# Earlier sums of squares in the handover, and four score banks with head-by-head maxima in the softmax attention of a language-model tower

## The reference

```python
hx = layernorm(h)
q, k, v = heads(hx @ Wq), heads(hx @ Wk), heads(hx @ Wv)      # 2 heads of 64
q = l2norm(q) * sqrt(64) * qn_g ;  k = l2norm(k) * sqrt(64) * kn_g
scores = where(causal, q @ k.T / sqrt(64), smallest)
o = softmax(scores) @ v ;  y = merge(o) @ Wo
gate = softmax(y @ gate_W + gate_b)                            # 8 experts
hid = gelu(y @ W1 + b1) ;  eo = hid @ W2 + b2                  # all experts, dense
out = h + sum(gate * eo)
```

## Time and profile before

| what | value |
|---|---|
| three runs | 873.12, 876.09, 878.2 us; median 876.09 |
| profiled execution, its own time | 872.14 us |
| its span | 870.3 us |
| busy shares of the span | PE 90%, DVE 82%, ACT 55%, POOL 39% |
| the chain that ended last | PE 78%, DVE 9%, issue 6%, ACT 5% |

### The profile page before, as it was taken

One profiled execution on the slowest core, in us unless ns is written; L12 is line 12 of the kernel. 1 busy time (PEld: TensorE's weight loads), 2 busy tenths in 40 slices (PEclk: granted clock), 3 DMA queues, 4 the chain that ended last, 5 costly groups with the idle time before them and its releaser, 6 DMA issues.

```text
span 870.3 us, 20958 instructions
## 1 busy us (share of the span) xinstructions
PE 785.4 (90%) x8188; PEld 556.7 (64%) x8188; DVE 709.8 (82%) x1588; ACT 479.3 (55%) x997; POOL 338.7 (39%) x379
## 2 busy tenths in 40 slices
PE   2699999999756688899999979999999999999997
PEld 1568887788523355555555556677777777777775
DVE  3558899888557766677676887999999999999997
ACT  2435555555234556677688865555555555555553
POOL 6639999777444456566467750000000000000000
PEclk9799999999879999999999999999999999999999
DMA  3101111000000000000000000000000000000000
GB/s 127 55 8 29 27 37 37 25 26 26 0 1 0 1 2 2 2 2 3 2 2 15 2 2 2 2 14 2 14 2 14 2 14 2 14 2 14 1 14 14
DMA packets 9666, 12.09 MB, mean 14 GB/s; under 512 B 1856, under 2 KB 6592, under 8 KB 9568
## 3 DMA queue, kind: packets, MB, share of 16 engines
q1 hardware_dynamic: 8544, 8.65, 3.4%
q0 software_dynamic: 1024, 2.10, 0.9%
HBM read 8.65 MB, written 2.10 MB: 12 GB/s over the span
## 4 chain that ended last, share of the span: by engine, by line
PE 78%; DVE 9%; issue 6%; ACT 5%; DMA 1%; POOL 1%; another core or an unknown queue 0%; DVEq 0%; ACTq 0%; POOLq 0%
PE ps L977 76%; DVE mx L825 1%; ACT qk L483 1%; ACT room L553 1%; DVE room L930 1%; DVE qkn L779 1%; DVE room L928 1%; ACT room L544 1%; DMA h_all<-emb_rows,idx 1%; DVE v L770 1%; DVE ss L764 1%; PE ps L1005 1%; DVE mx L820 1%; PE ps L985 0%; DVE och L901 0%
## 5 line engine op out<-in xcount | busy, mean ns | idle before, releaser
L568 ACT ACTIVATE cst<-ps,col 128x512 f32<-128x512 f32 x256 | 175.9, 688 | 164.1 <-PE ps L977 163.4
L977 PEld LDWEIGHTS ps<-arena,sq 128*128 128x128 f16 x3072 | 192.1, 98 | 61.8 <-DVE sq L961 4.3
L977 PE MATMUL ps<-arena,sq 128*128 128x128 f16 x3072 | 213.0, 219 | 0.5 <-DVE sq L961 0.5
L977 PE MATMUL ps<-y,arena 128*128 128x512 f16 x768 | 208.6, 381 | 1.3 <-DVE och L901 1.3
L961 DVE TENSOR_TENSOR sq<-cst,sq 128x512 f16<-128x512 f32 x256 | 176.2, 688 | 4.5
L364 POOL TENSOR_TENSOR room<-room 128x512 f16<-128x512 f32 (+3 forms) x119 | 121.1, 1034 | 82.3 <-ACT room L553 82.0
L956 DVE CAST sq<-cst 128x512 f16<-128x512 f32 x256 | 109.3, 427 | 11.6 <-ACT cst L568 4.2
L544 ACT ACTIVATE room<-ps 128x512 f32<-128x512 f32 (+3 forms) x160 | 76.7, 532 | 44.2 <-PE ps L977 42.9
L825 DVE TENSOR_REDUCE mx<-ps 128x2 f32<-128x1024 f32 (+2 forms) x64 | 70.2, 1096 | 37.6 <-PE ps L977 37.5
L977 PEld LDWEIGHTS ps<-y,arena 128*128 128x128 f16 x768 | 65.0, 98 | 34.2 <-issue 3.9
L977 PEld LDWEIGHTS ps<-v,room 128*128 128x128 f16 x1632 | 59.5, 99 | 40.5 <-issue 26.0
(11 more groups left out here) (154 smaller groups left out, 1172.6 us busy)
## 6 DMA issues: line engine op xcount, KB each, us to landing
sq<-w_rows SPq DMA_DIRECT2D x16, 256.0 KB
out<-h_all SPq DMA_DIRECT2D x32, 64.0 KB, 1.6
cst<-consts SPq DMA_DIRECT2D x1, 896.0 KB
h_all<-emb_rows,idx POOLq DMA_INDIRECT x32, 5.1
cst<-consts SPq DMA_DIRECT2D x1, 398.0 KB, 3.4
c<-consts SPq DMA_DIRECT2D x1, 256.0 KB, 5.5
wqkv<-w_qkv SPq DMA_DIRECT2D x1, 192.0 KB
wsm<-w_sm SPq DMA_DIRECT2D x1, 192.0 KB, 5.5
```

The lines of the kernel that those rows point to most:

```text
L568: a.activation(hid[:, f], ps[:, HBANK[f], :], ACT.Gelu_apprx_tanh, bias=col[:, K_B1 + k:K_B1 + k + 1], scale=1.0 / WS).then_inc(S["hid_rea ...
L977: return t_.matmul(o, l, r, start=start, stop=stop, skip_group_check=True)
```

## The change

In the handover DVE's step c now takes `sum_squares(c+1)` straight behind `unit_qk(c)`, where `sum_squares(c+2)` stood at the end of the step; `low_v(c+1)` stands last. POOL's factors follow at one chunk ahead, the coefficients of the last chunk are split by sequence into two groups of four (8 columns each, at c = 1 and 2), and the second masked product of that chunk goes ahead of `sum_squares(0)`. Pieces that finish the last chunk move one step later.

In the attention the exact scores go round four banks, 0, 1, 2, 5. All items are in `ALONE`: from item 3 on every head's rough scores go into bank 3, one after the other, with a reduction each, 128 in all in place of 64. `max_row` and the chain move to bank 4 (the last item's chain to 5). DVE takes a step's maxima ahead of its other work, and has 38 subtractions where it had 41: 20 in odd steps 19 to 61 with one part, 18 in the last 18 steps.

The core of the diff, which leaves out the waits that carry `bank5` over to a table `free` by bank:

```diff
@@ GpSimd @@
-                if c + 2 < NT:
-                    l2_factors(c + 2)
-                if c == 1:
-                    coefs(NT - 1)
+                if c + 1 < NT:
+                    l2_factors(c + 1)
+                if c in (1, 2):
+                    last_coefs(c - 1)
@@ ScalarE @@
-                        a.activation(p32[:, i % QR, lo:], ps[:, i % 3, lo:], ACT.Exp).then_inc(S["s_used"], 1)
+                        a.activation(p32[:, i % QR, lo:], ps[:, SBANK[i % 4], lo:], ACT.Exp).then_inc(S["s_used"], 1)
@@ VectorE @@
+            masked(NT - 1, 1)
             sum_squares(0)
-            masked(NT - 1, 1)
...
             def step_b(c):
                 unit_qk(c)
+                if c + 1 < NT:
+                    sum_squares(c + 1)
+                if c == 0:
+                    h1_out(NT - 2)
                 if c + 3 < NT:
                     normed2(c + 3)
-                if c == 0:
-                    sum_squares(1)
-                    low_v(1)
-                    h1_out(NT - 2)
...
-                if c + 2 < NT:
-                    sum_squares(c + 2)
-                    low_v(c + 2)
+                if c + 1 < NT:
+                    low_v(c + 1)
...
-                for part in MSLOT.get(s, ())[:1]:
+                two = MSLOT.get(s, ())
+                for part in two if two and two[0][0] > 2 else two[:1]:
                     row_max(*part, (0, 1))
@@ TensorE @@
             def lone_scores(it, r, kb, w, k, h):
...
-                if g < 10:
-                    pe.wait_ge(S["lo_ready"], NT - 1)
-                else:
-                    pe.wait_ge(S["sm_used"], g - 1)
+                pe.wait_ge(*free[bank])
...
-                guard = S["sm_used"], g + 1
+                free[bank] = S["sm_used"], g + 1
...
-                if s:
-                    pe.wait_ge(S["s_used"], 2 * s - 1)
+                if s >= 2:
+                    pe.wait_ge(S["s_used"], 2 * s - 2)
...
-                for part in lone[1:2]:
+                for part in lone[1:2] if len(lone) > 2 else ():
                     lone_scores(*part)
-                for part in pairs[:1]:
-                    pair_scores(*part)
                 if LAG <= s < NSTEP + LAG:
                     values(s - LAG, 1)
-                for part in lone[2:]:
+                for part in lone[2:3] if len(lone) > 2 else lone[1:]:
                     lone_scores(*part)
...
-                for part in pairs[1:]:
-                    pair_scores(*part)
+                for part in lone[3:]:
+                    lone_scores(*part)
@@ tables @@
-ALONE = (1, 2)
+ALONE = tuple(range(1, 8))
+SBANK = [0, 1, 2, 5]
+def chain_bank(m):
+    return 5 if m == len(ITEMS) - 1 else 4
+def lone_bank(it, g):
+    return 3 + g % 2 if it <= 2 else 3
```

More of the change, by code:

```diff
@@ L273, in coefs, with last_coefs @@
                                 ALU.subtract).then_inc(S["coef"], 1)
+            def last_coefs(b):
+                n = NT + b
+                pool.wait_ge(S["var_ready"], NT)
+                g.tensor_tensor(sm[:, 4, b], sm[:, 3, b], mhalf[:, 0:HA], ALU.pow).then_inc(S["r_ready"], 1)
+                pool.wait_ge(S["r_ready"], n)
+                g.tensor_tensor(sm[:, 5, b], sm[:, 4, b], row[:, R_NG:R_NG + HA], ALU.mult).then_inc(S["gr_ready"], 1)
+                pool.wait_ge(S["gr_ready"], n)
+                g.tensor_tensor(sm[:, 6, b], sm[:, 5, b], sm[:, 0, b], ALU.mult).then_inc(S["grmu_ready"], 1)
+                pool.wait_ge(S["grmu_ready"], n)
+                g.tensor_tensor(sm[:, 7, b], row[:, R_NB:R_NB + HA], sm[:, 6, b], ALU.subtract).then_inc(S["coef"], 1)
             def weights_low(n):
@@ L533, in out_part @@
                     act.wait_ge(S["gT_ps"], m + 1)
[L534 removed]
+                    a.activation(gT[:], ps[0:4 * E, chain_bank(m), 0:P], ACT.Copy, scale=WS).then_inc(S["gT_sb"], 1)
             max_row(0)
@@ L674, in outputs @@
             def outputs(c, cur, first=False):
-                dve.wait_ge(S["coef"], c + 1)
+                dve.wait_ge(S["coef"], c + 1 if c < NT - 1 else NT + 1)
                 dve.wait_ge(S["x_sb"], 2 * c + 2)
@@ L917, in _ @@
                         head_out(it)
+                for m in range(LAST):
+                    if s - YAT[m] in DVE_Y[:2]:
+                        out_part(m, DVE_Y.index(s - YAT[m]) + 3)
                 for i in (2 * s, 2 * s + 1):
@@ L931, in _ @@
                                         ).then_inc(S["plo_dve"], 1)
[L932 to L936, removed]
+                if two[1:] and two[0][0] <= 2:
+                    row_max(*two[1], (0, 1))
             dve.wait_ge(S["wlow_ready"], NPIECE)
@@ L1213, in lone_scores @@
                 if it == 2 and (r, kb) == (0, 0):
                     pe.wait_ge(S["hi_ready"], NT)
-                last = mm(ps[:, 3 + g % 2, 0:w], qh[half, q:q + P], kh[half, at:at + w], stop=kb < c)
+                last = mm(ps[:, bank, 0:w], qh[half, q:q + P], kh[half, at:at + w], stop=kb < c)
                 if kb == c:
                     for z in range(2):
-                        last = mask(ps[:, 3 + g % 2, w - P:w], z, h, neg_qk)
+                        last = mask(ps[:, bank, w - P:w], z, h, neg_qk)
@@ L1271, in scores @@
                         half = slice(h * DS, (h + 1) * DS)
-                        mm(ps[:, (2 * s + h) % 3, lo:], still[half, at:at + P], moving[half, q0 + lo:q0 + CH],
+                        mm(ps[:, SBANK[(2 * s + h) % 4], lo:], still[half, at:at + P], moving[half, q0 + lo:q0 + CH],
                            start=still is kh and moving is qh, stop=False)
@@ L1281, in scores @@
                     half = slice(h * DS, (h + 1) * DS)
-                    last = mm(ps[:, (2 * s + h) % 3, lo:], onehot[half], qm[half, it % 2, lo:], start=False)
+                    last = mm(ps[:, SBANK[(2 * s + h) % 4], lo:], onehot[half], qm[half, it % 2, lo:], start=False)
                 last.then_inc(S["s_ps"], 1)
             def out_part(m, j):
-                nonlocal bank5
+                bank = chain_bank(m)
                 if j == 1:
-                    pe.wait_ge(*bank5)
+                    pe.wait_ge(*free[bank])
@@ L1289, in out_part @@
                     pe.wait_ge(S["o_used"], m + 1)
                     for r in range(4):
-                        last = t_.transpose(ps[:, 5, r * P:(r + 1) * P], och[:, r], ident)
+                        last = t_.transpose(ps[:, bank, r * P:(r + 1) * P], och[:, r], ident)
                     last.then_inc(S["oT_ps"], 1)
-                    bank5 = S["oT_sb"], m + 1
+                    free[bank] = S["oT_sb"], m + 1
                 if j == 2:
-                    pe.wait_ge(*bank5)
+                    pe.wait_ge(*free[bank])
@@ L1311, in out_part @@
+                    free[bank] = S["gT_sb"], m + 1
                 if j == 5:
-                    pe.wait_ge(*bank5)
+                    pe.wait_ge(*free[bank])
                     pe.wait_ge(S["gT_sb"], m + 1)
                     for r in range(4):
-                        last = mm(ps[:, 5, r * D:(r + 1) * D], gT[:], b2s[:, r * D:(r + 1) * D])
+                        last = mm(ps[:, bank, r * D:(r + 1) * D], gT[:], b2s[:, r * D:(r + 1) * D])
                     last.then_inc(S["b2_ps"], 1)
-                    bank5 = S["h2_ready"], m + 1
+                    free[bank] = S["h2_ready"], m + 1
@@ L1343, in _ @@
                 lone = [(*part, h) for part in MSLOT.get(s, ()) if part[0] in ALONE for h in range(HS)]
-                pairs = [part for part in MSLOT.get(s, ()) if part[0] not in ALONE]
-                assert not (lone and pairs)
                 for part in lone[:1]:
@@ L1468, in on_pool @@
 def on_pool(i):
-    return i < 2 * 16 or (i % 4 != 3 if i < 2 * (NSTEP - 18) else i % 2 == 0)
+    s = i // 2
+    if s >= NSTEP - 18:
+        return i % 2 == 0
+    return i % 2 == 0 or len(MSLOT.get(s, ())) != 1 or s < 16 or s % 2 == 0
 def rounded(i):
```

72 lines of the change are left out of this document (34 added, 38 removed).

## The result

The changed kernel took 904.56 us (median of four runs, 897.89 to 905.45) against 876.73 for the kernel before: a ratio of 1.031, 95% interval 1.025 to 1.037. Slower was the forecast, but the size was not: 885, with 896 as the upper end of the range. The profiled execution took 905.45 us, its span 903.6, against 872.14 and 870.3.

What follows compares the result with a forecast made beforehand. A loop of waits bounds the handover, and PE is nearly full in the attention. Handover -17.5 and attention +26.5 make +9: own time 881.1, with 3.95 for the runs' median 885; range 866 to 896.

Steps and rivals of the forecast that it cites:

- Rival 1: Attention: single-head reductions release the bank earlier, PE's 9.6 us of waits go, median 849; chance 0.15.
- Rival 3: Handover: low clock or POOL's chain limits the gain to 8, steps 1 to 5 some 5.8, median 894; chance 0.13.
- the attention's sum: Attention, 325.5 to 478: time of the maxima's one bank adds to 178.4 against 152.5; attention +26.5 in all.
- the term for which PE's pieces leave the bank empty: Attention: the maxima's bank stands empty during 15 PE pieces at 1.0 and nine shorter ones, 18 us.
- the subtractions: Attention: 13 of VectorE's 20 odd-step subtractions, uncovered by PE's pieces, each delay the next head 0.75; 10 us.
- a risk of the handover alone: Handover: PE held at the low clock in more steps, some 6 projections at +1.4, gives 8 back.
- the bound of +36: Attention's upper bound: all 20 subtractions and every output meet a full bank.
- two of the forecast's signs: Attention: PE's waits for the reductions near 35 us where they were 9.6, and PE's busy share near 80%.
- The early steps: Attention's early steps: the chain in bank 4, which items 1 and 2 also use, costs +1.
- the handover's late steps: Handover, steps 6 to 13: PE and ACT leave the loop, 3.34 a step for 4.07; 27.6 for 33.4, gain 5.8.
- the first six steps: Handover, steps 0 to 5: counted one by one, 27.4 in place of 38.4; gain 12.1 with an earlier start of 1.1.
- The last term: End of the handover: pieces of the last chunk now end later, taking 0.4 off the gain.

Runs made afterwards that it cites:

- two banks: The changed kernel, but the heads alternate between banks 3 and 4, with the chain and maximum row in bank 5 and three score banks; 859.42 us.
- four and two: The changed kernel, but from item 3 on heads alternate between bank 4, shared with the chain and maximum row, and bank 3; 899.52 us.

## Why the prediction was wrong

**Right: what decides.** The maxima's one bank is a queue of one, and it costs more than the handover gives. A second bank for the maxima gave 859.42. The fourth score bank is worth nothing that could be measured (108.5 and 108.1 us in the steps at the full clock), as the earlier trace rows said. Rival 1, the halves that come sooner, fell: with a second bank the waits go to 1.7 us, with one they rise to 16.7. Rival 3 came nearer in time, 894, but not by its mechanism: of its long steps 1 to 5 only step 5 was over 5.5, and the handover gave 11.6 and not 8.

**Failed step: the attention's sum, the term for which PE's pieces leave the bank empty (18), and with it +26.5 for the attention.** The sum priced every piece of PE at the duration that it had at the high clock. In the stretch of 325.5 to 478 it came to 178.4; the changed kernel took 194.5 for the same steps. Head by head in its trace, bank 3's time from the first of the 128 products to the end of the last reduction, 195.1 us, is made up of

| part of the bank's time | forecast | measured |
|---|---|---|
| the reductions | 80.2 | 80.3 |
| from a product's start to its reduction's start | 72.5 | 73.7 |
| empty, from a reduction's end to the next product | 25.7 | 41.1 |

(forecast: 98 x 0.69 + 30 x 0.42; 128 x 0.43 + 10 + 7.5; 128 x 0.06 + 18). So the 18 was 33. The middle part came out by luck: the subtractions were twice too large, and a product at the low clock took 0.64 to its reduction and not 0.42 (medians). What the forecast left out in both is the low clock: 60 us more of it at 0.25 to 0.27, some 15 us, an estimate. Carried to no low clock at 0.27 us each, both forms with one bank (194.5 with 66 us low, 187.7 with 41) come to 176.5, an estimate from two points; so the queue itself was sized about right. Its price without the low clock shows in the 34 steps above, 108.5 us for the 97.1 of two banks. I had named the low clock as a risk of the handover alone, and the bound of +36 held none of it; the waits that I forecast for PE were the very thing that could bring it into the attention. For the same reason two of the forecast's signs failed: the waits were 16.7 us and not near 35, and PE's busy share was 90% and not near 80%, since slower work filled the time.

The falls come with the queue: the clock is 0.83 to 0.89 in the stretch with one bank and an unfilled PE, 0.90 and 0.94 where added products fill it, and 0.99 with two banks. That PE's idle moments cause the falls is shown as far as that; which of them does it is not shown.

The early steps, priced at +1, cost 2.6 (steps 0 to 6: 25.9 us for 23.3). Most of this goes with the clock too: PE ran low for 10 us there and 3 before, and two banks, with the same 10, took 25.1.

**Failed step: the handover's late steps, 27.6 for steps 6 to 13.** They took 287.90 - 258.44 = 29.5. The forecast took PE and ScalarE out of the loop; it had overlooked that `unit_qk` also waits for the transposes of the chunk before (`qkd_ps` in its row of the order), behind a projection in PE's list. Putting the transposes first, on PE and ScalarE together, gave the 3.34 of the forecast, so this step is shown.

**Mis-sized: the first six steps, 27.4.** They took 258.44 - 228.56 = 29.9. Steps 1 to 4 came to 16.45 us, forecast 17.0; steps 0 and 5 took 6.96 and 6.47 instead of 5.05 and 5.35. In both the product waits for PE; in step 5 a projection had taken 2.66 at the low clock. The last term is the way from the unit product of step 14 to the first exponential: 3.7 us for 2.1, where 0.4 more had been counted. PE waits 2.32 there for the low half of k.

## What to carry to other kernels

Count a bank as a resource of its own: from the first write to the reader's release, times its uses, plus every time it stands empty because PE is elsewhere; a reader that is far from full still makes PE wait if there is only one bank to write. Where a forecast makes TensorE wait more, price its work at both clock levels. And when an instruction moves up, go through all semaphores it waits for, not only the one that bound it before.

## What the runs showed of the hardware

Where one bank's queue and PE share the time, the low clock cost 0.25 us for each us at it (six steps of two kernels, 4.3 us for 17.4), not the half that a stretch bound by PE alone would give; between runs of one program it was 0.20 to 0.40. And a VectorE operation of only 128x32 took 1.12 us beside a GpSimd subtraction of 1.16 (the rows of the run "four and two"); its shortest in the changed kernel was 0.191. The bank's release hung on it, so the bank was held for that long. VectorE's roundings of 128x512 say the same: 0.41 to 0.43 us in the changed kernel where no GpSimd subtraction ran beside them, and up to 1.42 where one did.
